# Attention outputs and normalized rows of a transformer layer turned by DMA instead of by TensorE

## The reference

```
h   = layernorm(x)
q, k, v = h @ q_w.T, h @ k_w.T, h @ v_w.T            # per head [S, 128]
av  = softmax(causal(q k^T / sqrt(128))) @ v
out = av * sigmoid(q @ gate_w.T + gate_b)
x   = x + layernorm(out @ o_w.T)
h2  = layernorm(x)
f   = (silu(h2 @ G.T * gs) * (h2 @ U.T * us)) @ Dn.T * ds   # 5632 wide
x   = x + layernorm(f)
```

## Time and profile before

| | us |
|---|---|
| time before, median of 3 runs (1709.85 to 1791.71) | 1710.07 |
| profiled execution, its own time | 1707.6 |
| its span, slowest core (core 7, role B) | 1705.8 |
| spans of role A (cores 0, 2, 4, 6) | 1703.7, 1704.7, 1703.3, 1703.3 |
| spans of role B (cores 1, 3, 5, 7) | 1703.3, 1705.7, 1704.8, 1705.8 |
| PE busy, core 7 | 1653.5 (97%) |
| VectorE, ScalarE, GpSimd busy, core 7 | 657.6, 459.9, 127.5 |

### The profile page before, as it was taken

One profiled execution on the slowest core, in us unless ns is written; L12 is line 12 of the kernel. 1 busy time (PEld: TensorE's weight loads), 2 busy tenths in 40 slices (PEclk: granted clock), 3 DMA queues, 4 the chain that ended last, 5 costly groups with the idle time before them and its releaser, 6 DMA issues.

```text
span 1705.8 us, 29447 instructions; the slowest of 8 cores (1703.3 to 1705.8 us)
## 1 busy us (share of the span) xinstructions
PE 1653.5 (97%) x11631; PEld 1053.4 (62%) x11631; DVE 657.6 (39%) x1406; ACT 459.9 (27%) x724; POOL 127.5 (7%) x245
## 2 busy tenths in 40 slices
PE   3899999999999999999999999999999999999997
PEld 2656666666666666665445555555555557888854
DVE  5946565655655656562662111111111110121135
ACT  3744444444444444444222111111111110000012
POOL 0000000000000000000000000000000021111100
PEclk9999999999999999999999999999999999999999
DMA  9832222222131313034338544454545477555557
GB/s 240 242 56 51 51 38 51 38 39 50 26 63 26 63 26 51 1 62 112 148 125 153 87 87 87 87 92 82 94 80 91 82 126 123 91 93 90 91 142 232
DMA packets 44065, 152.13 MB, mean 89 GB/s; under 512 B 5136, under 2 KB 6288, under 8 KB 39312
## 3 DMA queue, kind: packets, MB, share of 16 engines
q0 software_dynamic: 34704, 102.81, 35.5%
q1 hardware_dynamic: 9216, 47.33, 8.5%
HBM read 238.24 MB, written 14.68 MB: 148 GB/s over the span
## 4 chain that ended last, share of the span: by engine, by line
PE 91%; DVE 4%; issue 2%; DMA 1%; ACT 1%; DVEq 0%; ACTq 0%; SPq 0%
PE psum L359 91%; DVE st L389 2%; DMA xin<-x_l 1%; PE psum L364 1%; DMA b_yb<-y_d 0%; DVE psum L638 0%; DVE b_xb L956 0%; ACT mv L372 0%; DVE mv L391 0%; ACT b_h1b L425 0%; DVEq L1338 0%; DVE b_yb L1225 0%; DVE mv L376 0%; ACT b_yb L1219 0%; ACT b_h1T L453 0%
## 5 line engine op out<-in xcount | busy, mean ns | idle before, releaser
L359 PE MATMUL psum<-b_h2T,b_fw 128*128 128x384 bf16 (+1 forms) x2752 | 521.1, 352 | 0.0
L359 PEld LDWEIGHTS psum<-b_h2T,b_fw 128*128 128x128 bf16 x2752 | 269.2, 98 | 251.1
L359 PE MATMUL psum<-b_h1T,b_wb 128*128 128x512 bf16 (+1 forms) x1536 | 387.1, 370 | 0.4 <-DVE b_Bb L557 0.4
L645 ACT ACTIVATE b_P<-psum 128x512 bf16<-128x512 f32 (+1 forms) x368 | 217.9, 592 | 382.6 <-DVE psum L638 312.1
L638 DVE TENSOR_TENSOR psum<-psum,b_Bb 128x512 f32<-128x512 f32 (+2 forms) x480 | 236.3, 511 | 133.0 <-PE psum L359 130.2
L359 PE MATMUL psum<-b_wb,b_h1T 128*128 128x256 bf16 x2048 | 271.2, 274 | 0.0
L359 PE MATMUL psum<-b_wd,b_hdn 128*128 128x256 bf16 (+1 forms) x2200 | 268.5, 285 | 0.0
L359 PEld LDWEIGHTS psum<-b_wd,b_hdn 128*128 128x128 bf16 x2200 | 215.3, 98 | 53.2
L1046 DVE SCALAR_TENSOR_TENSOR b_hdn<-psum,cf,b_sg 128x512 bf16<-128x512 f32 (+1 forms) x88 | 60.2, 684 | 463.3 <-PE psum L359 462.0
L359 PEld LDWEIGHTS psum<-b_wb,b_h1T 128*128 128x128 bf16 x2048 | 193.6, 98 | 28.9
L359 PEld LDWEIGHTS psum<-b_h1T,b_wb 128*128 128x128 bf16 x1536 | 141.2, 98 | 105.1 <-issue 0.8
(11 more groups left out here) (84 smaller groups left out, 856.4 us busy)
## 6 DMA issues: line engine op xcount, KB each, us to landing
b_fw<-wg_d POOLq DMA_DIRECT2D x43, 512.0 KB, 5.3
b_fw<-wu_d POOLq DMA_DIRECT2D x43, 512.0 KB, 6.1
b_wd<-wd_d POOLq DMA_DIRECT2D x66, 256.0 KB, 3.7
xin<-x_l SPq DMA_DIRECT2D x15, 1024.0 KB, 7.8
b_wb<-wv_d POOLq DMA_DIRECT2D x16, 512.0 KB, 7.2
b_wb<-wk_d POOLq DMA_DIRECT2D x16, 512.0 KB, 5.9
b_wb<-wq_d POOLq DMA_DIRECT2D x16, 512.0 KB, 5.2
b_xb<-x_l SPq DMA_DIRECT2D x7, 1024.0 KB, 5.3
```

The costliest lines, as they stand in the source:

```text
L359: return self.q.do("T", lambda e: e.matmul(out, lhsT, rhs, start=start, stop=stop, skip_group_check=True), waits, tok)
L645: te = self.q.do("S", lambda e: e.activation(p[:, 0:128 * n], self.bank(b, 128 * n), ACT.Exp, scale=CSC), [ta, self.av_tok.get(gi - PRING)])
```

## The change

Two transposes move from PE to SP's DMA queue. `q.dma` gets a flag `turn` that issues a transposing DMA, from SBUF to SBUF through the crossbar.

- In `close`, for heads 0 to 14, the DMA writes `avT` (two new buffers) from `avn`; the job in `small` is then only VectorE's multiply, due 7 calls after the close in place of 3. Head 15 keeps the old way. `close` number k now pops jobs until the multiply k-2 is out.
- In `o_norm`, one DMA per row tile turns `h2` (128x2048) straight into `h2T`, behind the spill and ahead of the next x load on SP's queue. `h2_turn`, its PE transposes and both copies are gone, and the feed forward waits on the DMAs.

```diff
-    def dma(self, chan, dst, src, waits=()):
+    def dma(self, chan, dst, src, waits=(), turn=False):
...
-        self.put(chan[0], lambda e: e.dma_start(dst, src), w, lane, 16)
+        self.put(chan[0], (lambda e: e.dma_start_transpose(dst, src)) if turn
+                 else (lambda e: e.dma_start(dst, src)), w, lane, 16)
...
-        while k >= 2 and k - 2 not in self.avn_tr:
+        while k >= 2 and k - 2 not in self.avt_free:
             self.small.pop(0)[3]()
...
+        c = slice(128 * x, 128 * (x + n))
+        th, avT = self.th[h % 2], self.avT[k % 2]
+        if h < H - 1:
+            self.avn_tr[k] = q.dma("Y", avT[:, 0:n, :],
+                                   avn[:, 0:n, :].rearrange("p t c -> p (t c)"),
+                                   [ev, self.avt_free.get(k - 2)], turn=True)
+
+            def job():
+                tg = q.do("V", lambda e: e.scalar_tensor_tensor(
+                    self.gat[:, h, c].rearrange("p (t c) -> p t c", c=128),
+                    th[:, c].rearrange("p (t c) -> p t c", c=128), 1.0,
+                    avT[:, 0:n, :], ALU.add, ALU.mult),
+                    [self.avn_tr[k], self.tok["th", h]])
+                self.avt_free[k] = self.gat_tok[h] = tg
+            self.small.append(("v", h, self.now + 7, job))
+            return
...
-            for n, (kc, c) in enumerate(order):
-                if t == 2 and n == 2 * KC:
-                    self.h2_turn(0, 4)
+            for kc, c in order:
...
-            if t > 1:
-                self.h2_turn(t - 1, 4 * ((t - 1) % 2))
             self.o_norm(t, sb, done)
...
-        self.h2_ok[t] = th
         self.spill[t] = q.dma("Y", self.d["y2"][t], xb[:, :], [ty])
+        self.h2_tr[t] = q.dma("Y", self.h2T[:, :, 128 * t:128 * t + 128],
+                              h2[:, :], [th], turn=True)
...
-        need = [self.h2_ev[t, hf] for t in range(a, a + n) for hf in range(2)]
+        need = [self.h2_tr[t] for t in range(a, a + n)]
...
-        for n, (i, g) in enumerate(early):
-            ready = self.ffn_mm(i, g)
-            if n == turn_at:
-                self.h2_turn(r.NQ - 1, 0)
-            self.ffn_act(i, g, ready)
-        self.tok["o_rest"] = [self.h2_tr[r.NQ - 1], *self.spill.values()]
+        for i, g in early:
+            self.ffn_one(i, g)
+        self.tok["o_rest"] = [*self.h2_tr.values(), *self.spill.values()]
```

More of the change, by code:

```diff
@@ L134 @@
     F_AT = [160768, 162816]
-    P_AT, AVN_AT, ABSQ_AT = 175104, 181248, 182784
+    P_AT, AVN_AT, ABSQ_AT, AVT_AT = 175104, 181248, 182784, 185088
     H1B = 36864
@@ L160 @@
     F_AT = [181248, 183296]
-    P_AT, AVN_AT, ABSQ_AT = 181248, 187392, 105472
+    P_AT, AVN_AT, ABSQ_AT, AVT_AT = 181248, 187392, 105472, 188928
     H1B = 107520
@@ L193, in __init__ @@
         self.o_done = range(14)
+        self.avt_free = {}
         self.small, self.now, self.rested, self.n_close = [], 0, 0, 0
@@ L228, in memory @@
         self.avn = [sb(f"avn{i}", [128, 3, 128], BF16, r.AVN_AT + 768 * i)
+                    for i in range(2)]
+        self.avT = [sb(f"avT{i}", [128, 3, 128], BF16, r.AVT_AT + 768 * i)
                     for i in range(2)]
@@ L695, in job @@
             self.avn_tr[k] = t
-            c = slice(128 * x, 128 * (x + n))
-            th, src = self.th[h % 2], self.bank(5, 64 * n).bitcast(BF16)
+            src = self.bank(5, 64 * n).bitcast(BF16)
             tg = q.do("V", lambda e: e.scalar_tensor_tensor(
@@ L701, in job @@
             self.bf[5] = [tg]
-            self.gat_tok[h] = tg
+            self.avt_free[k] = self.gat_tok[h] = tg
         self.small.append(("t", h, self.now + 3, job))
@@ L905, in out_proj @@
         q, r = self.q, self.r
-        self.xb_in, self.spill, self.h2_tr, self.h2_ev = {}, {}, {}, {}
-        self.h2_ok = {}
+        self.xb_in, self.spill, self.h2_tr = {}, {}, {}
         mv = self.k["mv"][3]
@@ L1063, in ffn @@
         early = [(i, g) for i in range(ni) for g in range(ng - 1)]
-        turn_at = len(early) - 2
         self.cast_to("wu", 2)
-        for n, (i, g) in enumerate(early):
-            ready = self.ffn_mm(i, g)
-            if n == turn_at:
-                self.h2_turn(r.NQ - 1, 0)
-            self.ffn_act(i, g, ready)
-        self.tok["o_rest"] = [self.h2_tr[r.NQ - 1], *self.spill.values()]
+        for i, g in early:
+            self.ffn_one(i, g)
+        self.tok["o_rest"] = [*self.h2_tr.values(), *self.spill.values()]
         self.ring, self.ring_at = [0, 1, 2, 3, 4, 5, 6, 7], 2 * ni
```

## The result

The changed kernel takes 1725.4 us in the median of 5 runs, the kernel before 1710.0 us; the ratio is 1.0084, 95% interval 1.0062 to 1.0106. It is slower by 14 us where I forecast 6 us less, and outside my range.

What follows compares the result with a forecast made beforehand. PE was taken to bound the kernel; role B saves 12.2 us of transposes and gives back 3.8, 1.5 and 1.0 us where the feed forward starts, 5.9 us net: 1704 us against 1710.0, range 1696 to 1716.

Steps and rivals of the forecast that it cites:

- What bounds the kernel, and what PE saves: Whole kernel: PE, 97% busy, sets the pace; removed transposes save 12.2 us in role B, 15.6 us in role A.
- the last turn: Start of the feed forward: the last h2 tile's DMA lands late, by 1.5 us in role B, 3 us in role A.
- Both are under 8 us: attention gives nothing back: Attention: avn turns take 4 us, up to 7 us beside a weight load, too short to cost PE time.
- the 8 us itself: Attention, role B: time from avn to landing beyond which PE is delayed, taken as about 8 us.
- Rival 3: Attention, role B: VectorE blocked at each head's multiply, 15 us per us beyond 8 us, 1740 us; chance 0.09.
- The start of the feed forward: Role B gives back 3.8 us for a weight load, 1.5 us for the last turn, 1.0 us for slow PE.
- the fourth load: Start of the feed forward: up weights of block 2 land 3.8 us after PE wants them.
- the pace: Start of the feed forward: PE comes back slow after waiting, at half pace for a few us, costing 1.0 us.
- my halves between the two queues: Start of the feed forward: the turn shares the DMA engines by halves from 907, costing the fourth load about 1.8 us.
- Rival 2: Start of the feed forward: last turn starves behind six loads, PE waits 12 us, 1710 to 1716 us; chance 0.15.
- Rival 4: Output projection: an h2 turn outlasts a tile's 13.8 us of PE, a backlog grows, 1774 us; chance 0.06.
- The sum for role B: Whole of role B: 12.2 - 3.8 - 1.5 - 1.0 = 5.9 us off, profiled execution from 1705.8 to 1699.9 us.

Runs made afterwards that it cites:

- first experiment: Changed kernel, but heads 13 and 14 are turned by PE again, so only heads 0 to 12 use the DMA: 1703.5 us, ratio 0.9972 to the kernel before.
- seventh experiment: Kernel before with only avn turned by DMA (heads 0 to 14), weight loads waiting for the last avn turn, h2 on PE: 1705.0 us, ratio 0.9976.
- fifth: Changed kernel with weight loads waiting for the last avn turn, and the last row tile's h2 turned by PE again: 1698.9 us, ratio 0.9941.
- sixth experiment: Changed kernel with weight loads waiting for the last avn turn, and block 3's two loads held until the last h2 turn lands: 1698.0 us, ratio 0.9936.
- fourth experiment: Changed kernel with plain DMA copies in place of the turns of avn and h2, contents wrong, only times count: 1715.9 us in one profiled execution.
- second experiment: Changed kernel, all turns kept, but each weight load after the first close waits for the last avn turn issued before it: 1704.8 us, ratio 0.9978.

## Why the prediction was wrong, by its steps

- *What bounds the kernel, and what PE saves*: right. 217 instructions less; the output projection gains 6.4 us on core 7 before the feed forward starts, where six tiles' transposes are 5.4 us. Role A (core 6) reaches its feed forward 15.4 us earlier (15.6 forecast, one tile included that comes later), and its start is 5.8 us longer; PE waits there for the last turn for 3.7 to 6.2 us (3 forecast).
- *"Both are under 8 us: attention gives nothing back"*: the step that failed, in both of its numbers. The first is the time of the turn. 4 us was too high for a turn alone (2.3), and 7 us was near beside two loads (7.3), but in heads 13 and 14 it was 10.8 and 13.7 us. The second is the 8 us itself. I worked it out from head 0 and took it for all heads of role B. The time from avn written to the landing, less PE's wait, gives the point from which PE pays:

| where | avn written to landing, us | PE waits, us | the point, us |
|---|---|---|---|
| head 11, core 7 | 7.4 | 0.3 | 7.1 |
| head 11, core 7, first experiment | 8.5 | 1.4 | 7.1 |
| head 11, core 5 | 9.0 | 1.9 | 7.1 |
| head 13, core 7 | 11.0 | 5.8 | 5.2 |
| head 14, core 7 | 13.8 | 11.4 | 2.5 |
| head 14, core 7, plain copy | 9.5 | 7.1 | 2.4 |
| head 14, core 7, seventh experiment | 3.5 | 1.1 | 2.4 |

  So 8 us was nearly right for an ordinary head and far too much for the last. In head 14 VectorE has no score additions left (PE adds head 15's bound itself) and comes to the multiply 0.6 us after avn is written. PE has few fillers left and stops 4.0 us after avn, for the reciprocal of the next close. Even the 4 us that I took for an undisturbed turn would have cost some 1.5 us there, an estimate from these rows. Why head 13 stands in between I haven't followed.

  What made the turns long was their company. I read GpSimd's queue in ordinary heads, where at most two loads fall on a close, and took them for the whole stage. The earlier trace rows end before 220 us. The timeline of GpSimd in the kernel before, core 7, shows what I hadn't asked for:

```profile
739.32 2.11 POOL L97 DMA_DIRECT2D b_wb<-wo_d  x4 [63.25 <-PE psum L359]
...
769.97 0.53 POOL L97 DMA_DIRECT2D b_wb<-wo_d  x1 [8.72 <-PE psum L359]
770.49 1.06 POOL L97 DMA_DIRECT2D b_wo<-wo_d  x2
771.52 0.56 POOL L97 DMA_DIRECT2D b_wg<-wg_d  x1
772.04 0.56 POOL L97 DMA_DIRECT2D b_wu<-wu_d  x1
```

Ten loads between 730 and 775 us, when the projections finish and free their buffers. In the changed kernel four and five of them fall on the closes of heads 13 and 14. That cost 19 us net. Holding only the loads, or only taking these heads off the DMA, gives it back: shown from both sides.
- *Rival 3* named this mechanism and its place on VectorE, with 0.09. Its price (15 us for each us beyond 8, once per head, 1740) was wrong. It happens in two heads of 15, and there each us beyond the point costs about one us; but the points are 5.2 and 2.5 us, so 3.0 and 5.8 us beyond 8 cost 5.8 and 11.4 us. (The 2.4 in its sum should be 10.5 - 8 = 2.5.)
- *The start of the feed forward*: the sum of 6.3 us was near (6.7 measured), and that is luck, for its parts weren't. I gave 3.8 us to the fourth load, 1.5 us to the last turn and 1.0 us to the pace. Measured: 1.3 us for weights, and those of block 1 rather than 2, 0.35 us before block 2, 3.4 us for the turn, 1.7 us for the pace. The norm ran 2.9 us earlier, as forecast: the spill is issued 4.6 us after the projection's end, 7.5 us before. The turn landed at 926.1, after the last of the loads (924.4); it hardly delayed them (the fourth landed after 15.6 us, 16.3 before), so my halves between the two queues were wrong. The fifth and sixth experiment show that the wait is the turn's.
- *Rival 2*: the last turn was late beside the loads, as it says, but PE waited 3.3 us for it and not 12.
- *Rival 4*: no backlog. A turn of h2 takes 4.3 to 6.0 us. The Trainium skill's 1309 ns per 128x128 block ("VectorE: DVE Perf Modes", The three transpose paths) can't be added up block by block: 16 blocks took 4.3 us, three 2.3 us. What the Trainium skill says in "Advanced Engine Details and Errata", X-Bar Transpose (TRN2), that transposing DMAs are as fast as others, agrees with the fourth experiment: 4.3 us turned, 4.1 us copied in the same pieces.
- *The sum for role B* would have been near the truth had the last heads been in it: the forecast span of 1699.9 and the 20.2 us that they gave back make 1720.1, and core 7 has 1720.1. That it fits so well is luck too: the output projection gained 1.0 us more than its transposes, the start gave 0.4 us more back, and 0.5 us were lost later.

## What to carry to other kernels

A transfer that an in-order engine waits for must be judged by its worst moment, not its median: list every burst on the other DMA queues in the whole stage, above all where a stage ends and buffers come free together, and set each against each new transfer. The time that a transfer may take is no constant of the program either: work it out where the stage runs dry, not only in its first round (7.1 us in head 11, 2.5 us in head 14). The cheap mend is on the side that has slack: loads wanted 20 us later can wait for the transfer wanted in 2 to 7. Where that isn't to be had, leave the few transfers that meet a burst on the engine that did the work before.

## What the runs showed of the hardware

- A crossbar turn of 96 KB from SBUF to SBUF lands in 2.3 to 2.4 us (32 KB: 2.2 us), one of 512 KB in 4.3 us, on otherwise idle engines; a plain copy (fourth experiment) takes 1.9 and 4.1 us.
- SP is occupied 1.1 to 1.3 us with the issue of most small turns (once 2.2 us). With a large one it is 1.4 to 3.8 us, and 10.0 us for the last, when the engines are loaded. The plain copies in their place occupied it 0.5 to 0.7 us, even the last.
- The turns appear as 256-byte packets on SP's queue, 128 for each 128x128 block. The queue's packets, MB and share on core 7, after:

```profile
q1 hardware_dynamic: 38656, 54.45, 10.7%
```

  Before it had 9216. The difference of 29,440 is 217 blocks x 128, plus 32 for each of 52 DMAs.
- After PE had waited 11.4 us it ran at half pace for some 3 us, granted clock 0.78 in 790 to 800 us. Four values matmuls of 129 columns and then the next matmul:

```profile
792.60 0.64 PE L364 MATMUL psum<-b_V,b_P 128*128 128x129 bf16 x4
793.03 0.53 PE L364 MATMUL psum<-b_qT,gwb 128*128 128x384 bf16 x1
...
795.21 0.39 PE L364 MATMUL psum<-b_V,b_P 128*128 128x129 bf16 x4
795.43 0.38 PE L364 MATMUL psum<-b_qT,b_kT 128*128 128x512 bf16 x1
```

  From start to start the 516 columns take 0.43 us and, 3 us later, 0.22 us, the paces of 1.2 and 2.4 GHz. (The lengths, 0.64 and 0.39 us, also hold a latency.)
- After a wait of 3 to 4 us the lower pace is there or not. 16 matmuls of 384 columns, 2.60 us from start to start at full pace, took 3.95 us on core 7 after 3.3 us, 5.08 us on core 6 after 3.7 us, and 2.60 us on core 7 of the second experiment after 4.0 us. The last two:

```profile
667.51 5.28 PE L364 MATMUL psum<-a_h2T,a_wg 128*128 128x384 bf16 x16 [3.69 <-DMA a_h2T<-a_h2b]
672.59 3.09 PE L364 MATMUL psum<-a_h2T,a_wu 128*128 128x384 bf16 x16
...
909.18 2.76 PE L366 MATMUL psum<-b_h2T,b_wg 128*128 128x384 bf16 x16 [3.97 <-DMA b_h2T<-b_h2b]
911.78 2.76 PE L366 MATMUL psum<-b_h2T,b_wu 128*128 128x384 bf16 x16
```
